# One MLP unit and the first output tile moved one to three steps later in a cross-attention chunk, and its GELU split into two instructions

## What is computed

```python
h = _layernorm(x, ln1_g, ln1_b)
x = x + _mha(h, h, ...)                # self attention, 16 heads of 16
h = _layernorm(x, ln2_g, ln2_b)
x = x + _mha(h, context, ...)          # cross attention, 1601 keys
h = _layernorm(x, ln3_g, ln3_b)
h = gelu(h @ mlp_w1.T + mlp_b1) @ mlp_w2.T + mlp_b2    # 256 -> 1024 -> 256, exact GELU
return x + h
```

## Time and profile before

| | us |
|---|---|
| median of 3 runs | 1571.6 |
| lowest, highest | 1568.4, 1571.73 |
| profiled execution, its own time | 1572.35 |
| its span, first to last instruction | 1570.7 |
| PE busy, ACT busy, DVE busy | 1468.8, 1072.1, 536.5 |
| mean granted TensorE clock | 0.972 |

### The profile page before, as it was taken

How to read it: one execution, slowest core, us unless ns; L and a number is a source line. 1 busy time by engine, 2 the same in 40 slices (tenths; PEclk the granted TensorE clock), 3 DMA queues, 4 the chain that set the end, 5 groups by cost and what they waited for, 6 DMA issues and landing times.

```text
span 1570.7 us, 20677 instructions
## 1 busy us (share of the span) xinstructions
PE 1468.8 (94%) x8094; PEld 644.5 (41%) x8094; DVE 536.5 (34%) x1296; ACT 1072.1 (68%) x1297; POOL 41.7 (3%) x58
## 2 busy tenths in 40 slices
PE   8889989999867999999999999899999999999998
PEld 5467757757632222322322322232232432332346
DVE  1535545545553022230331332233232142133222
ACT  2323333333325999999999999798788797788852
POOL 2100000000001000000000000000000000000000
PEclk9999999999968999999999999899899999999999
DMA  7400010010016800010010056401000100000000
GB/s 218 171 7 7 8 57 19 8 67 5 31 53 125 139 22 11 11 40 22 11 38 13 19 77 115 102 19 61 13 12 11 35 12 11 18 18 1 2 13 14
DMA packets 36651, 64.22 MB, mean 41 GB/s; under 512 B 6464, under 2 KB 22656, under 8 KB 35808
## 3 DMA queue, kind: packets, MB, share of 16 engines
q1 hardware_dynamic: 31184, 41.40, 12.1%
q0 software_dynamic: 5360, 21.37, 3.8%
HBM read 40.85 MB, written 22.02 MB: 40 GB/s over the span
## 4 chain that ended last, share of the span: by engine, by line
PE 75%; ACT 17%; DVE 4%; issue 3%; DMA 1%; POOL 0%; DVEq 0%; SPq 0%; ACTq 0%; POOLq 0%
PE PS L1006 22%; PE PS L989 16%; ACT PX L713 14%; PE PS L827 6%; PE PS L836 6%; PE PS L1057 4%; PE PS L1067 3%; PE PS L1042 2%; PE PS L778 2%; PE PS L877 2%; PE PS L813 2%; PE PS L753 2%; PE PS L845 1%; PE PS L848 1%; PE PS L782 1%
## 5 line engine op out<-in xcount | busy, mean ns | idle before, releaser
L713 ACT ACTIVATE PX<-PS 128x1024 f32<-128x1024 f32 (+1 forms) x928 | 883.8, 1040 | 138.6 <-PE PS L989 87.4
L1006 PE MATMUL PS<-PX,V 128*32 128x512 f32 (+1 forms) x3712 | 501.0, 612 | 5.0 <-ACT PX L713 3.1
L989 PE MATMUL PS<-QST,stack 50*128 50x512 f32 (+1 forms) x1856 | 386.0, 473 | 20.0 <-issue 14.0
L989 PEld LDWEIGHTS PS<-QST,stack 50*128 50x128 f32 (+1 forms) x1856 | 156.3, 186 | 421.7 <-ACT PX L713 340.2
L1006 PEld LDWEIGHTS PS<-PX,V 128*32 128x32 f32 (+1 forms) x3712 | 74.1, 109 | 152.3 <-issue 126.9
L1448 DVE COPY OT<-PS 128x512 f32<-128x512 f32 x32 | 22.1, 692 | 309.6 <-PE PS L1006 308.3
L652 ACT ACTIVATE PR<-PS,small 128x1601 f32<-128x1601 f32 x16 | 25.5, 1596 | 117.0 <-DVE small L1324 117.0
L827 PE MATMUL PS<-tokF,XT 128*128 128x512 f32 (+1 forms) x256 | 93.2, 518 | 4.2 <-DVE small L1305 3.6
L836 PE MATMUL PS<-tokT,PT 128*128 128x256 f32 (+1 forms) x416 | 93.3, 382 | 0.6 <-DVE CZ L1374 0.6
L836 PEld LDWEIGHTS PS<-tokT,PT 128*128 128x128 f32 (+1 forms) x416 | 78.0, 191 | 10.6 <-issue 0.8
L659 ACT ACTIVATE TR<-PS,small 128x128 f32<-128x128 f32 x32 | 10.0, 363 | 85.8 <-PE PS L848 85.8
(11 more groups left out here) (146 smaller groups left out, 1187.4 us busy)
## 6 DMA issues: line engine op xcount, KB each, us to landing
QST<-q_parts SPq DMA_DIRECT2D x192, 64.0 KB
q_parts<-PARTS POOLq DMA_DIRECT2D x16, 512.0 KB, 3.4
stack<-k_parts SPq DMA_DIRECT2D x24, 200.1 KB, 6.8
stack<-k_parts SPq DMA_DIRECT2D x18, 256.0 KB
k_parts<-KPARTS POOLq DMA_DIRECT2D x8, 512.0 KB, 3.2
v_cross<-V POOLq DMA_DIRECT2D x1, 3328.0 KB, 10.0
V<-v_cross SPq DMA_DIRECT2D x2, 1664.0 KB, 13.0
k_parts<-PARTS POOLq DMA_DIRECT2D x6, 512.0 KB, 3.2
```

What stands on the lines that cost most here:

```text
L713: act.activation(PX[0:kr, (2 * t + half) % 4, :, :], PS[0:kr, slot:slot + 2, :], ACT.Exp, scale=SCALE).then_inc(at["exp"], 1)
L989: ins = pe.matmul(PS[0:kr, 2 * (n % LOOK) + jj, :], KST[a][lo:lo + NROW, pair, kt * P:kt * P + kr].bitcast(F32R), QST[lo:lo + NROW, pair, ...
L1006: ins = pe.matmul(PS[32 * j:32 * j + 32, 6, :], V[0:kr, kt, 2 * (g // 2 * GH + j) + g % 2, :], PX[0:kr, (2 * t + j // 2) % 4, j % 2, :], s ...
```

## The change

In the table, the last MLP unit (7) moves from step 35 to step 37, both its parts. The first output tile's four parts move from steps 37, 37, 39, 39 to 38, 38, 40, 40. All other entries stay. ACT's GELU becomes two instructions: the first seven units (128x3584) as soon as they have been written, then the last (128x512) once it has been; only the second tells PE. It all stays at step 36 in ACT's order.

```diff
-    {"y": [5, 7, 9, 11], "h": [17, 18], "m": list(range(19, 27)) + list(range(29, 35)) + [35, 35],
-     "o": [37, 37, 39, 39, 42, 42, 43, 43, 45, 45, 46, 46, 48, 48, 49, 49]},
+    {"y": [5, 7, 9, 11], "h": [17, 18], "m": list(range(19, 27)) + list(range(29, 35)) + [37, 37],
+     "o": [38, 38, 40, 40, 42, 42, 43, 43, 45, 45, 46, 46, 48, 48, 49, 49]},
...
             def gelu(q):
 
+                early = HID // P - 1
+                act.wait_ge(at["unit_taken"], HID // P * q + early)
+                act.activation(HIDT[:, 0:early], HIDT[:, 0:early], ACT.Gelu)
                 act.wait_ge(at["unit_taken"], HID // P * (q + 1))
-                act.activation(HIDT[:], HIDT[:], ACT.Gelu).then_inc(at["gelu"], 1)
+                act.activation(HIDT[:, early:], HIDT[:, early:], ACT.Gelu).then_inc(at["gelu"], 1)
```

## The result

The changed kernel takes 1580.5 us (median of 5, 1579.1 to 1585.3) against 1571.7 for the kernel before (1568.4 to 1573.7): a ratio of 1.0063, 95% interval 1.0042 to 1.0084. It is slower by 8.8 us by the medians and 9.9 us by the ratio, where 4.8 were forecast, and lies just above the upper end of the range, 1580.5. Each ratio in this document is against executions of the kernel before that were timed alongside; of 36 such executions beside e1 to e4, two in a slow state (1691 and 2022 us, at a mean granted clock of 0.83 and 0.65) are left out, so 34 count there.

A forecast was written before the change was run, and what follows sets the result against it. PE, busy 94% of the span, was taken to bound the kernel. Hole +1.13 and the stretch to pv(40) +0.45 made 1.6 us a GELU, 4.8 for three: 1576.4 us, range 1570.5 to 1580.5.

The forecast's parts named there:

- (e): Behind unit 7, PE stands before scores(77) until exp(74) ends: hole 4.2 us instead of 3.26, +1.13 us a GELU.
- (a to d): Up to the GELU's end: exp(73) 1.35 us earlier, unit 7 ready 0.2 us early, GELU parts 3.18 and 0.59 us.
- The waits behind the hole: Between scores(77) and pv(40): scores(78) waits 0.58 us for exp(75), pv(39) 0.37 us for DVE's copy.
- The clock: Behind the hole, up to pv(40): the clock falls each time, costing 1.3 us a GELU, with ends 0 and 2.8.
- Long stretches: Rival, chance 0.10: behind the hole each GELU gets 6.8 us at half clock, slower, 1580.8 us.
- The clock stays up: Rival, chance 0.18: the clock holds at the later-starting hole at the GELU, no change, 1572.4 us.
- The hole swallows unit 7: Rival, chance 0.07: PE finds work at the GELU's end, the hole shrinks, 5.3 us faster for three, 1566.3 us.
- The reload costs more: Rival, chance 0.03: the table load before exp(74) takes twice its 1.283 us, +3.8 us, slower, 1580.2 us.

The follow-up runs named there:

- e1: The kernel before with only the GELU split into the change's two instructions: 1573.1 us, ratio 1.0003.
- e4: The kernel before with six useless matmuls in its 3.26 us hole, ahead of the half tile: 1572.8 us, ratio 1.0000.
- e3: The changed kernel with the first output tile back in steps 37, 37, 39, 39, ahead of scores(77): 1567.0 us, ratio 0.9967.
- e2: The changed kernel with six useless matmuls in the hole behind unit 7: 1573.6 us, ratio 1.0008.
- e9: The changed kernel with the whole first output tile in step 37, its first half released by the GELU's first part: 1562.4 us, ratio 0.9932.

## Why the prediction was right or wrong

The direction and the mechanism were right; the size, 4.8 us, was about half of what came (8.8 by the medians, 9.9 by the ratio), because one term of the sum, the cost of the clock, was taken at half its measured size.

*The order, and what is late next (e).* Right. The hole was forecast at 4.2 us and is 4.00. From the end of pv(34) to scores(77) it took 9.55 us where before had 8.55 to the half tile: +1.00 for +1.13. e3 shows the cause: with the tile ahead of scores(77) and all else equal the loss becomes a gain of 5.2 us.

*exp(73), unit 7, the GELU's length (a to d).* Right. The two parts take 3.190 and 0.612 us (3.18 and 0.59), unit 7 was there 0.14 us before it was needed (0.2), and e1 puts the split at 0.1 us (0.155).

*The waits behind the hole.* The wait before scores(78) was 0.55, 0.32, 0.32 us in the change and 0.55 to 0.56 in e2 at full clock (0.58); the one of pv(39) for DVE's copy 0.68, 0.31, 0.31 (0.37). Right, but for the first chunk, whose copy came later.

*The clock.* This is the term that failed: "The unknown is the clock. ... I take 1.3", of ends 0 and 2.8. e2 against the change measures 2.8 us a GELU. I had moved the three stretches of before back by the 0.9 us by which the hole is longer, keeping their lengths of 6.8, 3.4 and 3.4. What the runs show in its place is 6.8 us nearly every time. After the hole PE no longer begins with half a tile; it has scores, a wait, scores and pv. In six passes of the change the stretch was 6.8 us five times, and was 3.4 only where the fall came 1.0 us after PE had gone on. With the half tile first (before and e1) it was 3.4 in all four passes in which the fall came 0.17 to 0.73 us after, and 6.8 in the two in which it came 1.4 and 1.5 us ahead. Two of them, both of e1:

```profile
1481.90:1485.30 3.40, 3.40 (x10) 2.22 (x10) 0.00 (x0) 3.39 (x4) 0.00 (x0) 0.50 0.00 0
1348.90:1352.20 3.30, 3.30 (x10) 1.82 (x9) 0.00 (x0) 3.29 (x5) 0.00 (x0) 0.50 0.00 0
```

So a length seen behind one order and one hole was carried over to another. That the order behind the hole makes the difference is argued and not shown: the hole too is longer, 4.00 us for 3.26 and 3.36, and no run has the longer hole with the half tile first. With 2.8 for 1.3 and 1.0 for 1.13 the sum is 3 x (1.0 + 2.0) = 9 us, between the 8.8 and 9.9 that were measured.

The rival *Long stretches* was therefore the case that came true: it was priced at 1580.8 and given 0.10. The range ended at 1580.5, below that price, and that is why it missed a result that the text had worked out. *The clock stays up* was wrong where it matters, but e2 shows its price to be right (1573.6 for 1572.4). *The hole swallows unit 7* was right in its condition: PE goes on 2.4 us after the GELU's end in the change, and where it goes on after 0.14 us, in e3, the kernel gains; it is 5.2 us faster for the 5.3 of the rival, though that is in part luck: of the 1.92 us a GELU that e3 gains on PE only 1.25 come before the half tile (7.3 for 8.55), and the rest is the clock, which the rival did not count. *The reload costs more* did not happen: the loads are 1283 ns, and the first exponential starts 1.29 us after the load does, which leaves no room for the drain that the Trainium skill adds to a switch of tables (ScalarE: Activation LUTs, What ACT_TABLE_LOAD costs).

## What to carry to other kernels

When a wait's hole is to be filled, look at what stood at its far end: here the piece that was pushed away had itself been covering a table load and an exponential, and was worth more than the piece put in. Fill with the work that depends on nothing behind the slow engine, and keep the matmuls that the wait releases right behind it (e9: 9.4 us faster than before). The holes of 3.26 to 6.90 us at the GELU had half clock in or behind them in every pass of every profile here, so such a hole is to be priced with it; and the price, 0.7 us a GELU before and 2.8 in the change, could not be taken over from one order of work to the other.

## What was not expected

Useless matmuls in the hole of the change made it 7 to 9 us faster (e2), and the same in the hole of before gained nothing in the total (e4), although every GELU was 0.67 us shorter; part of the half clock seems to have come back elsewhere. The clock stayed low for 6.8 us with the half tile behind two score groups and for 3.4 with it ahead of them, for falls at nearly the same moment after PE went on (0 to 0.52 us, and 0.17 to 0.73); the hole differed too, 4.00 us against 3.26 and 3.36. DVE's copy after pv(38) of the first of the three chunks started 0.37 us later against its pv than in the other two, before (0.50 against 0.13 us) and after; no run here tells why.
